# A routed feed-forward layer in three parts: part sizes, scatters and single expert tiles

## The reference

```
logits = h @ gate_w.T + expert_bias
topk_logits, topk_idx = top_k(logits, 2)
topk_w = softmax(topk_logits)
y = silu(h @ w1[e].T) @ w2[e].T            # for each chosen e < 8
out = sum(topk_w * y) + w_zero * h
x = x + gb * out
```

## Time and profile before

| | |
|---|---|
| median of 3 runs | 2662.19 us (2661.35 to 2664.83) |
| profiled execution, its own time | 2662.52 us |
| its span in the profile | 2660.6 us |
| attention and the stages before it | to about 1961 us |
| `route` | to 2151.2 us |
| `experts` | to 2660.6 us |
| tiles in `experts` (adds to the output) | 122 |
| mean granted clock of TensorE | 0.963 |

### The profile page before, as it was taken

The page is one execution under the profiler, slowest core; times in us unless marked ns, Lnnn a source line. Parts: engine busy times, 40 slices in busy tenths (PEclk is TensorE's granted clock), DMA queues, the critical chain, the costliest instruction groups (busy, mean ns, idle before and its releaser), DMA issues. The chain is left out here.

```text
span 2660.6 us, 47761 instructions
## 1 busy us (share of the span) xinstructions
PE 2485.4 (93%) x16108; PEld 1291.7 (49%) x16109; DVE 1909.7 (72%) x3231; ACT 1665.4 (63%) x2989; POOL 764.7 (29%) x896
## 2 busy tenths in 40 slices
PE   6987889999999999999999999999989579999998
PEld 4554233333333333333333333333348478889897
DVE  5987768788788788787787887887638455456543
ACT  2666357777777777777777777777764254444554
POOL 2545201121121111111111111111214737657544
PEclk8998789999999999999999999999999689999999
DMA  5798633253332433432432432320247556457465
GB/s 177 207 251 224 123 78 87 67 110 85 92 83 83 94 88 83 92 90 78 97 90 73 101 81 56 74 59 19 69 131 216 191 130 125 101 97 131 90 102 76
DMA packets 225081, 286.06 MB, mean 108 GB/s; under 512 B 29526, under 2 KB 178550, under 8 KB 224502
## 3 DMA queue, kind: packets, MB, share of 16 engines
q1 hardware_dynamic: 185596, 235.80, 35.0%
q0 software_dynamic: 32160, 41.57, 9.1%
q10 hardware_dynamic: 7136, 6.32, 0.7%
HBM read 143.64 MB, written 139.08 MB: 106 GB/s over the span
## 5 line engine op out<-in xcount | busy, mean ns | idle before, releaser
L238 DVE TENSOR_REDUCE mxc<-ps 128x2 f32<-128x1024 f32 (+4 forms) x1168 | 1298.1, 1149 | 316.0 <-PE ps L226 166.6
L1186 ACT ACTIVATE probs<-ps 128x512 f32<-128x512 f32 (+1 forms) x2240 | 1177.6, 588 | 462.1 <-PE ps L1143 450.5
L1159 PE MATMUL ps<-probs,vs 128*32 128x512 f32 (+3 forms) x5120 | 599.5, 541 | 1.3 <-POOL probs L1076 1.2
L1143 PE MATMUL ps<-qs,ks 99*128 99x512 bf16 (+3 forms) x1760 | 504.4, 352 | 14.1 <-DMA qs<-m_t 9.3
L226 PE MATMUL ps<-ks,qs 96*128 96x512 bf16 (+3 forms) x1760 | 464.9, 355 | 25.3 <-DVE mxc L238 17.4
L1076 POOL TENSOR_SCALAR_AFFINE_SELECT probs<-probs 128x512 f32<-128x512 f32 x256 | 161.7, 635 | 870.4 <-ACT probs L1186 870.4
L1143 PEld LDWEIGHTS ps<-qs,ks 99*128 99x128 bf16 x1760 | 147.6, 97 | 380.2 <-ACT probs L1186 271.0
L1874 PE MATMUL ps<-x_t,w_at 128*128 128x128 f32 x2000 | 251.8, 280 | 15.3 <-ACT x_t L1915 11.3
L1874 PEld LDWEIGHTS ps<-x_t,w_at 128*128 128x128 f32 x2000 | 247.4, 196 | 28.3 <-issue 23.1
L1998 POOL DMA_INDIRECT out<-ys,idx x122 | 194.3, 1593 | 207.3 <-DMA out<-ys,idx 92.5
L226 PEld LDWEIGHTS ps<-ks,qs 96*128 96x128 bf16 x1760 | 163.6, 99 | 179.7 <-DVE mxc L238 42.6
(11 more groups left out here) (172 smaller groups left out, 2195.8 us busy)
## 6 DMA issues: line engine op xcount, KB each, us to landing
ks<-k_parts SPq DMA_DIRECT2D x66, 256.0 KB, 4.1
qs<-q_parts SPq DMA_DIRECT2D x66, 256.0 KB, 4.1
xs<-slot_x SPq DMA_DIRECT2D x128, 131.0 KB
v_ones<-vout SPq DMA_DIRECT2D x64, 256.0 KB, 3.6
vs<-v_ones SPq DMA_DIRECT2D x64, 256.0 KB, 3.2
attn_t<-o_sb SPq DMA_DIRECT2D x64, 256.0 KB, 2.9
slot_x<-zero SPq DMA_DIRECT2D x48, 262.0 KB, 2.5
q_parts<-parts SPq DMA_DIRECT2D x96, 128.0 KB, 2.7
```

Of the source, the lines that this page charges most:

```text
L238: return dve.tensor_reduce(mxc[:, h0:h0 + nh, i, c], unit_view(ps, u, at), AX_X, ALU.max)
L1143: ins = pe.matmul(o[:, h, :], ks[r][0:SROWS + MROWS, h0 + h, j * P:(j + 1) * P], qs[r][0:SROWS + MROWS, h0 + h, J * QJ + lo:(J + 1) * QJ], ...
L1159: ins = pe.matmul(o_ps[SLOT * g:SLOT * (g + 1), lo:QJ], vs[:, r, j, SLOT * g:SLOT * (g + 1)], probs[:, (NKT * r + m) % NPB, g, 0:QJ - lo], ...
L1186: act.activation(probs[:, (NKT * r + m) % NPB, h0:h0 + nh, 0:QJ - lo], st_view(r, s), ACT.Exp, scale=DH ** -0.5).then_inc(exp_done, 1)
```

## The change

Parts of 16, 20 and 28 tiles take the place of 24, 24 and 16, so `NPAIR` becomes 20, 24 and 32. `SCATTERING` goes from 6 to 8: of the 32 scatters of part 0, 24 stand behind the last eight multiplications and 8 follow in one row (before: 18 of 48, and 30 in one row). The lags of part 1's stages are raised so that its work stays in the same steps. `route` then has 32 scatters and `experts` 96, where it was 48 and 80.

Each part now counts its used tiles in two numbers, the first and the second tiles of the pairs, and each tile has its own branch. A part with an odd number of tiles no longer works on an empty one. ScalarE gets one more wait at the start of a part, on its own copies.

```
-PARTS = [24, 24, 16]
+PARTS = [16, 20, 28]
...
-SCATTERING = 6
+SCATTERING = 8
...
-    s.mark(dve.tensor_scalar(last[:, :], tend[:, E - 1:E], 1.0, None, ALU.add))
+    for j in range(2):
+        s.mark(dve.tensor_scalar(last[:, j:j + 1], tend[:, E - 1:E], float(1 - j), None, ALU.add))
...
-                blocks((6, counts(0, 2)), (7, counts(1)), (0, output), (3, logits), (8, weights(0, 1)), (2, normed), (8, weights(1, E)))
+                blocks((6, counts(0, 2)), (10, counts(1)), (0, output), (3, logits), (8, weights(0, 1)), (2, normed), (8, weights(1, E)))
...
-                       (5, chosen(0, 2)), (6, placed(0, 2)), (7, zeros), (6, chosen(1)), (8, placed(1)))
+                       (5, chosen(0, 2)), (6, placed(0, 2)), (7, zeros), (9, chosen(1)), (11, placed(1)))
...
-                blocks((1, deviation), (1, normalise), (5, shares(0, 2)), (7, shares(1)), (2, normed), (8, weights))
+                blocks((1, deviation), (1, normalise), (5, shares(0, 2)), (10, shares(1)), (2, normed), (8, weights))
...
-        def pairs_used(eng, p):
-            return eng.value_load(r["npair"][0:1, p, 0:1], min_val=0, max_val=NPAIR[p])
+        def tiles_used(eng, p):
+
+            return [eng.value_load(r["npair"][0:1, p, j:j + 1], min_val=0, max_val=NPAIR[p]) for j in range(2)]
 
         def pair(eng, i, used, body):
-            with eng.If(used > i):
-                for q in range(2):
+            for q in range(2):
+                with eng.If(used[q] > i):
                     body(2 * i + q, q, i)
...
+                    if p > 0:
+                        act.wait_ge(w1_done[p - 1], used[p - 1][0] + used[p - 1][1] + 2)
+                        apart(act)
                     copy_w1(0, 0)
```

More of the change, by code:

```diff
@@ L186, in build @@
             r["turn"] = c2.enter_context(nc.sbuf_tensor("turn", [P, NPARTS, HT], I32))
[L187 removed]
+            r["npair"] = c2.enter_context(nc.sbuf_tensor("npair", [P, NPARTS, 2], I32))
             for n, w in {"tri": P, "ones": P, "iota_e": ET, "iota_t": HT, "spare": NT}.items():
@@ L1449, in route @@
         cmp, eidf = hn[:, :, :].rearrange("p j c -> p (j c)")[:, 0:HT * E].rearrange("p (t e) -> p t e", e=E), sb("eidf_all", [P, HT])
-        last, turned = sb("last", [P, 1]), sb("turned_at", [P, HT])
+        last, turned = sb("last", [P, 2]), sb("turned_at", [P, HT])
         wt_done, wt_copy = sem("wtr"), sem("wtc")
@@ L1851, in _ @@
                     if p > 1:
-                        sp.wait_ge(tx_done[p - 2], 2 * used[p - 2] + 2)
-                        sp.wait_ge(meta_done[p - 2], 2 * used[p - 2] + 2)
+                        sp.wait_ge(tx_done[p - 2], used[p - 2][0] + used[p - 2][1] + 2)
+                        sp.wait_ge(meta_done[p - 2], used[p - 2][0] + used[p - 2][1] + 2)
                     load(0, 0)
                     load(1, 1)
-                    used.append(pairs_used(sp, p))
+                    used.append(tiles_used(sp, p))
                     pairs(sp, p, used[p], body)
@@ L1892, in _ @@
                     if p > 0:
-                        pe.wait_ge(xt_done[p - 1], 2 * used[p - 1] + 2)
+                        pe.wait_ge(xt_done[p - 1], used[p - 1][0] + used[p - 1][1] + 2)
                     turn_x(0, 0, 0)
                     if p > 0:
-                        pe.wait_ge(silu_done[p - 1], 2 * used[p - 1] + 1)
+                        pe.wait_ge(silu_done[p - 1], used[p - 1][0] + used[p - 1][1] + 1)
                     up(0, 0)
@@ L1899, in _ @@
                     if p > 0:
-                        pe.wait_ge(y_done[p - 1], 2 * used[p - 1] + 2)
+                        pe.wait_ge(y_done[p - 1], used[p - 1][0] + used[p - 1][1] + 2)
                         apart(pe)
-                    used.append(pairs_used(pe, p))
+                    used.append(tiles_used(pe, p))
                     pairs(pe, p, used[p], body)
@@ L1929, in _ @@
                     if p > 0:
-                        with act.If(used[p - 1] > 0):
-                            act.wait_ge(down_done[p - 1], 2 * used[p - 1])
+                        with act.If(used[p - 1][0] > 0):
+                            act.wait_ge(down_done[p - 1], used[p - 1][0] + used[p - 1][1])
                             apart(act)
@@ L1934, in _ @@
                     copy_x(1)
-                    used.append(pairs_used(act, p))
+                    used.append(tiles_used(act, p))
                     pairs(act, p, used[p], body)
@@ L1978, in _ @@
                     meta(1)
-                    used = pairs_used(dve, p)
+                    used = tiles_used(dve, p)
                     for i in range(NPAIR[p]):
@@ L1999, in body @@
                                                 compute_op=ALU.add).then_inc(add_done[p][q], 16)
-                    used = pairs_used(pool, p)
+                    used = tiles_used(pool, p)
                     n, told = 0, not later[p]
@@ L2014, in _ @@
                     assert told
[L2015 to L2018, removed]
+                    for q in range(2):
+                        with pool.If(used[q] > 0):
+                            pool.wait_ge(add_done[p][q], 16 * used[q])
+                            apart(pool)
                     for q in range(2):
```

## The result

The changed kernel takes 2667.73 us (median of 20 runs, 2663.86 to 2676.94) where the kernel before takes 2662.94 in as many: a ratio of 1.0018, 95% interval 1.001 to 1.0025. That is 4.8 us slower, at the edge of what counts as no change; 2669.0 was predicted, and +6.8. The profiled execution has a span of 2663.6 us against 2660.6, 3.0 more.

What follows compares the result with a forecast made beforehand. It took the scatter row to bound the end of `route`, GpSimd pairs with two token tiles, TensorE part 2. Route -23 plus experts +29.8 gave +6.8 on 2662.2, 2669.0 us; range 2652 to 2686.

Steps and rivals of the forecast that it cites:

- Route, -23: End of `route`: a shorter row of scatters lets it end at 2128.1 against 2151.2, 23 us earlier.
- the release: End of `route`: the held engines go on between the scatter row's end, 2099.9, and 4.8 us later; taken as 2103.
- The rival that something else held them until 2131: `route`: the stall isn't the row's doing, so it ends about 10 us earlier at best; 2682 and more, chance 0.06.
- Experts, +29.8: `experts`: the three parts sum to 519.7 us against 489.9, though there is a tile less; the addition is GpSimd's.
- GpSimd's line: Part 0: GpSimd's work from the first silu to `x_ready`, 143.6 us, then 8.2 us to part 1's first silu.
- the 0.43 us a pair: Parts 0 and 1: time missing per pair from GpSimd's sum in the old part 0, added for 15 and 18 pairs.
- The sum of adds, scatters, zero terms and borders: Part 0: GpSimd's line from the first silu through pair 14, before the per-pair addition, 137.1 us.
- The rival of held signals in `experts`: Parts 0 and 1: TensorE waits for signals while the ring runs dry; +42 for `experts`, about 2682, chance 0.20.
- its own sign: Parts 0 and 1: the prediction is wrong if they stay under 145 and 172 us, or their unnamed waits grow.
- Its +42: `experts`, held-signals rival: growth of 42 us in place of 29.8.
- The ring hides GpSimd: `experts`: nothing is missing per pair, growth only 14 to 17 us, net -6 to -13, about 2653; chance 0.27.
- A branch for each tile, nothing: `experts`: one more branch per used pair is covered by the matmuls, adding nothing.

Runs made afterwards that it cites:

- the row of 24: Changed kernel plus 24 useless scatters in a row in part 2, and later 24 memsets; silus fell back 27.7 us at the scatters, 11.8 at the memsets.
- the eight scatters: Changed kernel plus eight useless scatters at four places of part 2, three with memset pauses; silus fell back 10.4 us without pauses, 7.6, 2.2 and 5.0 with.
- the row that waits for each tile: Kernel before, with GpSimd waiting behind every second scatter of the row ending `route` until both landed; ratio 1.0051 to the kernel before.
- the bursts of memsets: Changed kernel plus useless work in part 2: four scatters behind each of pairs 1 to 8, four memsets behind 13 to 20; memset pairs kept 7.5 us.
- the last kernel: Parts of 20, 20 and 24, spread scatters, single tiles, plus a 250-column memset behind each scatter of `route`'s row; 2628.99 us, ratio 0.9984 to the kernel before.

## Why the prediction came out right, and where it wasn't

**Route, -23: right, -25.1 measured.** Two more blocks with scatters were to cost 1.6 and cost 1.4 (last multiplication at 2082.8 against 2081.3); the release was put at 2103 and came at 2101.7; TensorE's counts kept VectorE 1.2 us in place of 4.4, where I had 0.9. That the unbroken row of scatters is what holds the engines up is shown three times: by the row of 24 against memsets, by the eight scatters with and without pauses, and by the row that waits for each tile. The rival that something else held them until 2131 is out. What in the chip does it, and that it is the signals, is inferred from waits that go on after their values were made.

**Experts, +29.8: right in size, +27.7 measured** (517.6 less 489.9, from the first silu to the last). Part 0 was put at 151.8 and took 146.4, part 1 at 178.7 and 181.5, part 2 at 189.2 and 189.7.

By the traces the whole change is +3.0, and by the medians +4.8. The total came out well partly by luck: part 0 was put 5.4 us too high and part 1 2.8 too low, for the reasons below.

**Part 0: GpSimd's line sets it, as predicted, and the step that failed is the 0.43 us a pair.** The sum of adds, scatters, zero terms and borders was 137.1; the last add of that sum ends at 140.3, so 3.2 us are missing in place of the 6.4 that I added. From there to the first silu it was 6.1 in place of 8.2, as the loads go out 2.1 us before the profile has that add end. The 0.43 was no loss per pair. In the old part 0 the waits before the adds of that sum, counted beyond the usual 0.30, are 25.5 us, and my sum has 16.8 (the second add and five borders at 2.8); the difference of 8.7 is nearly all of the 9.1 that was missing. Nine adds waited 2.1 to 3.1 us there, and I had counted six. I also took the row at the 42nd add, one pair behind the one that releases `x_ready` by `due`, and in a part that TensorE ended. The new part 0 has the four long waits that I counted for it, two of them longer, 4.4 and 4.3 us. With single tiles and the scatters spread, the old part's 42nd add ends at 164.8 us from the first silu in place of 179.2, with 10.7 us of such waits, since a scatter then lies between two adds that must follow each other. How much of the 14.4 is held signals, which also go there, isn't told apart.

**Part 1: the size is near, the end isn't as predicted.** Its last add before `x_ready` ends 166.8 us in, against 162.8 by the bare sum and 170.5 with the 0.43; then I had 8.2 us to the first silu, and it was 14.8. Three adds follow, and TensorE ends the part, 8.0 us behind the loads. A line of GpSimd's alone doesn't give 181.5.

**The rival of held signals in `experts` had a part of the mechanism, at the wrong price.** I said the prediction would be wrong if unnamed waits grew: they grew from 40.5 to 99.9 us, so by its own sign the prediction's account of these parts falls short, though its time is near and GpSimd's line does end part 0. The rival asked for some ten scatters in a row; four between the adds do it, with 40.3 us of unnamed waits beside 32 scatters in part 2. Its +42 was also too high by its own terms: 121 tiles at 3.71, 51 us for the pairs with two token tiles and two borders of 13.3 give +37. Why it came to +28 I can only argue: in parts 0 and 1 GpSimd's line is nearly as long as the parts, so that held signals and its own work lie beside each other and don't add up. Spreading the scatters takes 7 us from the new parts and leaves 80.7 of unnamed waits. How much of part 1's 181.5 is theirs isn't settled.

**The ring hides GpSimd: wrong.** `experts` grew by 27.7 and not by 14 to 17. The ring puts off some 9 us, as the bursts of memsets show, and TensorE waits 5.7 us for the loads at the end of part 0. But one thing that this rival said holds: nothing is missing per pair.

**A branch for each tile, nothing: right,** 3.71 us a tile in part 2 with and without. The Trainium skill (Runtime: NRT & Kernel Launch, section Instruction fetch mechanics) warns that a taken branch beyond the fetched window stalls the engine. No such stall shows in part 2 of these runs, and the new parts with pairs are 7.7 us slower than with single tiles, where 60 branches at 0.4 us would make them 13 faster. What I didn't see is that in the old parts the single tiles don't show in the total: of two tiles fewer, the one in part 2 counts in the trace, and parts 0 and 1 take 6.2 us more together, for a reason that is open.

**Why a large change moved so little.** It takes 22 scatters from a row that held everybody, 16 into `experts` and 6 behind multiplications; 25 us come back in the one stage and 28 go in the other, where parts of 16 and 20 tiles put more scatters behind fewer adds. With spread scatters the old parts are 0.33% faster than the new: the row in `route` costs less than the same scatters in crowded parts of `experts`.

## What to carry to other kernels

When an engine issues indirect transfers beside the others' work, count not only its time but its rests. Longer work without transfers set the others back less here (15.0 us against 22.7) and gave no unnamed wait. Before moving transfers to another stage, try to spread them so that short gaps are left. And before a term is carried over from one part to another, look which engine ends each: the loads that go out before TensorE wants them say that it isn't the one that releases them.

## What was not expected of the hardware

- In every trace but the last kernel's, scatters of 0.96 us with 0.30 between them held other engines' waits somewhere. The longest on ScalarE was 9.4 us with eight in a row, 21.4 with 24 and 29.6 with 33; the engines went on between 4.5 us before the row's end (one silu in the row of 24) and 5 us behind it. In the one place that was tried with 0.6 us of something else behind each of eight scatters there was no such wait.
- Memsets in a row (24.4 us, against 30.1 for the scatters) held nothing.
- One chip ran the kernel before 31 us faster, and in the one trace taken there no wait of `route`'s end or of `experts` is unnamed. Whether that is the chip or something else about that measurement is open.
